# Second attention of a four-stage kernel: the multiplication of probabilities by inverse sums on GpSimd instead of VectorE

## What is computed

```python
q = q * cos + _rotate_half(q) * sin
k = k * cos + _rotate_half(k) * sin
scores = jnp.einsum('bhqd,bhkd->bhqk', q, k) / sqrt(HD) + bias
scores = jnp.where(causal, scores, jnp.float32(-1000000000.0))
attn = jax.nn.softmax(scores, axis=-1)
ctx = jnp.einsum('bhqk,bhkd->bhqd', attn, v)
```

## Time and profile before

| | us |
|---|---|
| median of 3 runs | 2512.11 |
| lowest and highest of them | 2511.95, 2513.39 |
| the profiled execution's own time | 2515.83 |
| its span in the profile | 2513.9 |
| second attention, first QK of batch 0 to the experts' first norm | some 1907 to 2228 |

### The profile page before, as it was taken

How to read it: one execution, slowest core, us unless ns; L and a number is a source line. 1 busy time by engine, 2 the same in 40 slices (tenths; PEclk the granted TensorE clock), 3 DMA queues, 4 the chain that set the end, 5 groups by cost and what they waited for, 6 DMA issues and landing times.

```text
span 2513.9 us, 81640 instructions
## 1 busy us (share of the span) xinstructions
PE 2312.5 (92%) x34944; PEld 1575.0 (63%) x34944; DVE 1766.0 (70%) x2707; ACT 1373.6 (55%) x2778; POOL 1598.5 (64%) x931
## 2 busy tenths in 40 slices
PE   5668999999999999999999999999987988889998
PEld 3435666666666666666666666666655766656665
DVE  2348788877888778887788778887756888832232
ACT  1115666666666666666666666666644666643332
POOL 0039889888898888888888888988843222201111
PEclk8879999999999999999999999999987899989999
DMA  4001111111121112211121112211122000000000
GB/s 111 0 9 37 30 35 51 49 43 30 34 58 50 33 32 51 53 37 31 33 62 48 33 30 58 52 33 35 30 58 64 1 1 1 1 1 5 5 5 5
DMA packets 77303, 83.91 MB, mean 33 GB/s; under 512 B 24964, under 2 KB 48786, under 8 KB 76946
## 3 DMA queue, kind: packets, MB, share of 16 engines
q1 hardware_dynamic: 76946, 78.70, 12.2%
HBM read 26.56 MB, written 1.07 MB: 11 GB/s over the span
## 4 chain that ended last, share of the span: by engine, by line
PE 49%; DVE 29%; issue 12%; ACT 7%; POOL 3%; SPq 0%; ACTq 0%; DMA 0%; POOLq 0%; DVEq 0%
PE bank L613 7%; DVE n L1222 6%; DVE qk L1215 6%; PE bank L532 5%; ACT qk L908 4%; PE bank L625 4%; PE sbank L569 3%; PE bank L633 3%; DVE sh L1235 3%; DVE mx L1231 3%; PE bank L821 2%; PE obank L831 2%; PE sbank L831 2%; PE obank L602 2%; PE sbank L821 2%
## 5 line engine op out<-in xcount | busy, mean ns | idle before, releaser
L1215 DVE TENSOR_TENSOR qk<-bank,tab 128x1024 f32<-128x1024 f32 x384 | 469.2, 1222 | 212.5 <-ACT qk L908 212.4
L1528 POOL TENSOR_TENSOR qk<-qk 128x1024 f32<-128x1024 f32 x192 | 454.3, 2366 | 188.5 <-DVE qk L1215 188.3
L1532 POOL TENSOR_TENSOR rn<-n2m,cst 128x16 f32<-128x16 f32 x192 | 562.8, 2931 | 16.0
L532 PE MATMUL bank<-wqk,xs 128*128 128x512 f32 x768 | 409.2, 615 | 2.6 <-DMA xs<-Z 0.9
L908 ACT ACTIVATE qk<-bank 128x512 f32<-128x512 f32 x384 | 226.5, 590 | 300.5 <-PE bank L532 300.5
L1536 POOL TENSOR_TENSOR qk<-qk,rn 128x1024 f32<-128x1024 f32 x192 | 365.4, 1903 | 28.1 <-POOL rn L1532 0.9
L543 PEld LDWEIGHTS bank<-cst,qk 128*128 128x128 f32 x1536 | 191.5, 141 | 215.6 <-issue 170.4
L1540 POOL TENSOR_TENSOR lnr<-lnv,cst 128x2 f32<-128x2 f32 (+1 forms) x88 | 66.4, 754 | 394.1 <-DVE lnv L1110 394.1
L543 PE MATMUL bank<-cst,qk 128*128 128x128 f32 x1536 | 231.8, 274 | 11.3 <-POOL qk L1536 11.3
L1222 DVE TENSOR_REDUCE n<-qk 128x16 f32<-128x1024 f32 x192 | 232.1, 1209 | 0.0
L553 PE MATMUL lnbank<-wv,xs 128*64 128x512 f32 x768 | 208.0, 620 | 0.0
(11 more groups left out here) (201 smaller groups left out, 4332.6 us busy)
## 6 DMA issues: line engine op xcount, KB each, us to landing
vp<-vp SPq DMA_DIRECT2D x672, 65.0 KB, 2.0
wqk<-in_L_ffn_Wqkv SPq DMA_DIRECT2D x24, 256.0 KB, 3.7
wv<-in_L_ffn_Wqkv SPq DMA_DIRECT2D x6, 512.0 KB, 4.0
wo<-in_L_ffn_Wo SPq DMA_DIRECT2D x6, 512.0 KB, 4.2
xs<-Z SPq DMA_DIRECT2D x48, 64.0 KB, 2.0
xs<-Z SPq DMA_DIRECT2D x48, 63.8 KB, 2.7
vp<-in_L_ffn_w SPq DMA_DIRECT2D x1, 2048.0 KB, 13.1
mw<-in_L_ffn_w SPq DMA_DIRECT2D x8, 256.0 KB, 6.9
```

The costliest lines, as they stand in the source:

```text
L532: nc.tensor.matmul(bank[s % 2][:, :], xs[:, odd, WIN + r * P:WIN + r * P + P], wqk[:, lo:lo + 512], start=True, stop=True).then_inc(p_full, 1)
L1215: tt(qk[:, both, :].rearrange("p o (h d) -> p o h d", d=DH), heads(bank[c % 2][:, :]).unsqueeze(1).broadcast_to([P, 2, PAIRS, DH]), table. ...
L1528: tt(direct, direct, swapped, ALU.add).then_inc(sum_done, 1)
L1532: tt(rn[:, m % 2, :], n2m[:, :], const("mhalf"), ALU.pow).then_inc(rn_done, 1)
```

## The change

`normalise3` on DVE keeps only the reciprocal, and has a new wait ahead of it: `pn` of job m - 2, since POOL reads the same buffer of `rdn`. The multiplication stands in a new `normalise3` on POOL, which waits for the reciprocal (`rdn`). POOL's `step3` becomes a loop over the slots: in slot m first the multiplication of job m - 1, then in slots 1 and 4 the inverse roots of the next batch's norms, in slot 8 the first `mask_q`, in slot 11 the inverse root for the batch before, in slot 12 the second `mask_q`. The lists of PE and ACT don't change.

```diff
@@ VectorE
                 dve.wait_ge(s3["px"], NJ * b + m + 1)
+                wait(dve, s3["pn"], NJ * b + m - 1)
                 nc.vector.reciprocal(rdn[:, m % 2, 0:n], dn[:, m % 2, 0:n]).then_inc(s3["rdn"], 1)
-                dve.wait_ge(s3["rdn"], NJ * b + m + 1)
-                part = px[:, m % 2, :].rearrange("p (h n) -> p h n", h=n)
-                tt(part, part, rdn[:, m % 2, 0:n].unsqueeze(2).broadcast_to([P, n, P * (r + 1)]), ALU.mult).then_inc(s3["pn"], 1)
@@ GpSimd
+            def normalise3(b, m):
+                r, hs = JOBS[m]
+                n = len(hs)
+                pool.wait_ge(s3["rdn"], NJ * b + m + 1)
+                part = px[:, m % 2, :].rearrange("p (h n) -> p h n", h=n)
+                tt(part, part, rdn[:, m % 2, 0:n].unsqueeze(2).broadcast_to([P, n, P * (r + 1)]), ALU.mult).then_inc(s3["pn"], 1)
+
             def step3(b, next_batch, batch_before):
                 u = 3 * b + (LN_S3 + 1)
-                if next_batch:
-                    for n in range(2):
-                        inverse_deviations(S, (u if batch_before else LN_S3 + 2) + n)
-                    mask_q(b + 1, 0)
-                if batch_before:
-                    inverse_deviations(S, u + 2 if next_batch else u)
-                if next_batch:
-                    mask_q(b + 1, 1)
+                for m in range(NJ + 3):
+                    if 1 <= m <= NJ:
+                        normalise3(b, m - 1)
+                    if next_batch and m in (1, 4):
+                        inverse_deviations(S, (u if batch_before else LN_S3 + 2) + m // 4)
+                    if next_batch and m == 8:
+                        mask_q(b + 1, 0)
+                    if batch_before and m == 11:
+                        inverse_deviations(S, u + 2 if next_batch else u)
+                    if next_batch and m == 12:
+                        mask_q(b + 1, 1)
```

## The result

The changed kernel takes 2523.85 us (median of five runs, 2522.88 to 2525.17); beside it the kernel before took 2513.21. The ratio is **1.0044**, with a 95% interval of 1.003 to 1.0059: slower by 0.44%, or 10.6 us. The forecast was 2521.7.

What follows compares the result with a forecast made beforehand. Neither PE nor DVE is full, both near it, each waiting for the other. Batches 1 to 6 +7.6, batch 0 0, batch 7 +2.0: +9.6 us on 2512.1 gives 2521.7; range 2507 to 2535.

Steps and rivals of the forecast that it cites:

- The price: Moved multiplication: 1.04 us on POOL, estimated from L1536, against 0.69 on DVE; ends 0.95 and 1.27.
- The latency: Reciprocal to T: 1.32 to 1.33 us against 0.94, so 0.39 us later wherever PE waits for it.
- the upper rival: Longer multiplication (1.27 us, some 7.5 times per batch, +3.0 per batch) or lower clock: 2532 us; chance 0.20.
- The lock in slot 2: L1334 held by POOL's multiplication until 2037.36: DVE's 0.7 us lead gone, T of job 2 at +0.42.
- The queue: Slots 8 to 13: T of job 8 waits behind mask_q (+0.61), T of job 11 behind the inverse root (+1.26).
- The clock: PE's idle times before T of jobs 8 and 10 may lower its clock; shares a rival's chance of 0.20.
- Batch 0: No finish covers mask_q, so T of job 8 comes later still; batch ends at -0.8, taken as 0.
- if PE's clock doesn't fall: Condition on batch 0 ending at -0.8; PE's clock was 0.88 there against 0.96.
- batch 7: Last batch, no mask_q and no preparation: every second T waits, five times 0.39, +2.0 us.
- the full-clock part: Step-by-step sum without a clock change: +1.26 us per batch, over batches 1 to 6 +7.6.
- The step for slots 7 and 8: L1350 no longer held (1.40 to 0.42) and L1383 of 1.08 us gone: add of slot 8 at -0.99.
- The faster rival: DVE bounds, latency hidden: 3.4 us less per batch against three T waiting 0.39 more; 2497 us; chance 0.15.

Runs made afterwards that it cites:

- e2: Changed kernel plus one small unused GpSimd instruction (0.25 us) between the wait for the reciprocal and every job's multiplication; 2536.53 us.
- e3: Kernel before, multiplication on VectorE, but the first mask_q of a batch waits until job 7 is normalised; 2502.43 us, ratio 0.9962.
- e1: Changed kernel with the two halves of the first mask_q split over slots 8 and 9 instead of both in slot 8; 2510.24 us, ratio 0.9992.
- e5: e1 plus an unused reduction of 0.69 us on VectorE behind every reciprocal, giving back the load the change took; 2509.08 us.
- e6: e3, and the second mask_q of a batch also waits, until job 11 is normalised; 2499.19 us, ratio 0.9947.
- e8: e6 with the multiplications of jobs 5 and 6 alone on GpSimd; 2499.13 us.

## Why the prediction was right, and where it was off

The forecast of slower by 9.6 us met 10.6. Its parts, each against its measurement:

- **The price.** 1.04 us forecast for the multiplication, 1.039 measured; the sum of two whole operands of the same size takes 1.27. Whether the broadcast factor makes the difference, or the product instead of the sum, no run separates.
- **The latency.** From reciprocal to T 1.33 us, as forecast (job 7 of batch 3: 2057.94 to 2059.27), and seven to eight such places in a chain: e2 gives 7 to 8. But this is the price of a further delay in the changed kernel, not of the move. From e3 to e1, batch 4, the move costs 1.24 us, where 7.5 times 0.39 would be 2.9: in e3 T waits at four jobs only, in e1 at seven, and the chain changes sides on the way. Against e3 the adds of e1 fall behind by 0.4 us each ahead of slots 5, 7 and 9 and by 0.66 at the end, and win back 0.1, 0.2 and 0.25 us ahead of slots 3, 6 and 8. The forecast went step by step and counted what DVE wins back; the upper rival multiplied a further delay by 7.5, and that is what e2 measures.
- **The lock in slot 2.** L1334 held, 1.05 instead of 0.42 us. The add behind it came 0.10 us earlier than before instead of 0.03 later: the held sum ended 0.28 us after GpSimd's instruction, not 0.42. All later slots of the forecast are pessimistic by these 0.13 us or a little more: +0.25 for the add of slot 5 (forecast +0.42), +0.44 for slot 7 (+0.59), -1.20 for slot 8 (-0.99).
- **The queue.** T of job 8 behind `mask_q`, T of job 11 behind the inverse root: seen as forecast. From the first add to the next batch's +1.26 was forecast, +0.99 measured at full clock. The experiments split it: -1.38 for the later `mask_q` (38.59 to 37.21, e3), +1.24 for the multiplication on GpSimd with its new list (37.21 to 38.45, e3 to e1), +1.13 for the queue (e1 to the changed kernel). The sum is +0.99.
- **The mis-sized terms.** The clock stood among the rivals, not in the sum: the lower clock at the end of a batch costs 0.9 to 1.2 us in batches 1 to 4. The kernel before loses by it too, which the steps took as they stood in batch 3 (its add of slot 2 comes at 5.77 us, against 5.07 at full clock). Net of that the clock adds 2.6 us over batches 1 to 6. Batch 0, forecast at 0, came out 1.26 us longer (41.71 for 40.45): T of job 8 waits 2.63 us there, and PE's next PV and QK run at the lower clock (1.08 and 2.08 us), which the forecast had put under "if PE's clock doesn't fall". Batches 1 to 6 took 8.5 us longer in all for 7.6; batch 7 1.5 for 2.0. With 0.6 us at the stage's start that puts the stage's last add 11.9 us later. The spans differ by 7.4 us only: the rest, 4.5 us less, lies behind the stage, where the two programs are the same and the changed kernel's profile has the higher granted clock (0.95 against 0.93); and the profiled execution of the kernel before was 2.6 us above its median. So that the total came so close is in part luck: the full-clock part was 0.3 us per batch too high, and the clock, which the sum left out, made up for it.
- **The reason for the gain.** The step for slots 7 and 8 gave part of its gain to the multiplication of 1.08 us that left DVE. From slot 7 to slot 8 the adds are 4.57 us apart before, 2.93 in the changed kernel, and 3.19 in e3, with that multiplication still on DVE: 1.38 of the 1.64 us is `mask_q`, and 0.26 at most the multiplication that left; by e5, which gives DVE its load back (3.04), it is 0.11. So the hold on L1350 was rightly named, but of what the step put down to the L1383 that is gone, the larger part, 0.39 us, was the hold as well.
- **The faster rival.** It said that the change wins if T of job 8 doesn't wait for `mask_q`. e1 has that, and is only as fast as the kernel before: the condition wasn't enough. The rival counted three T that wait longer, and in e1 T waits for GpSimd at seven jobs of batch 4; the DVE time that it counted as gain, e5 prices at 0.1 us a batch.

Left open: why the add of slot 2 or the end of a batch runs at the lower clock in some batches of a kernel and not in others (e6 has one such batch, e8 two, the changed kernel four of its batches 1 to 6 at their end). The same instructions in the same order precede them.

## What to carry to other kernels

Before work moves to an idle engine, count how often its result is waited for. Here the move itself, with 0.39 us more latency for each of twelve jobs, cost 1.24 us a batch; once made, every further delay was paid seven to eight times a batch, while twelve times 0.66 us of work on VectorE cost 0.1 us. The two prices hold around the changed kernel and don't add up to that of the move. Look also at what already stands in the list of the engine that takes it: 3.75 us of work with no hurry, put ahead of a result that PE waits for, cost 1.1 us, and in four of the batches 1 to 6 again as much through PE's clock. The best part of the change was the place that it gave to `mask_q`: one wait on GpSimd, which keeps its long instructions away from VectorE's sums of two SBUF inputs, gives it without moving anything (e3 0.4%, e6 0.5% faster).

## What the hardware showed unexpectedly

A sum on VectorE that GpSimd's instruction held ended 0.28 us after that instruction's end (L1334 from 2041.47 to 2042.52, the multiplication from 2041.20 to 2042.24), though it takes 0.42 us alone. It is the same for every held instruction of the stage in the kernel before, the changed one and e3: L1334, L1350 and L1361, of 256 columns, end 0.28 us after GpSimd's, and L1383, of 512 columns and 0.69 us alone, ends 0.55 us after it. Both are 0.14 us less than the instruction takes alone. Either VectorE does the first 0.14 us under the hold, or GpSimd's record ends 0.14 us after it lets go; no run separates the two. For an estimate it is enough: a held instruction ends at the end of GpSimd's, plus its own time, less 0.14 us. The Trainium skill, page "SBUF — State Buffer", section "Who interferes with whom", calls what the two engines share an exclusive lock; the hold of 0.63 us agrees with that.

And PE's idle times can cost a second time. After waits of 0.91 and 1.15 us within a batch PE's next 3 us of work took 0.9 to 1.2 us longer, at the lower of its two clock levels (1.2 instead of 2.4 GHz) for part of them, behind batches 1 to 4 of the changed kernel; after the same two waits in batches 5 and 6 it didn't.
